# Second attention of a two-layer kernel: when the input's maximum and q's turn are issued, and which engines scale the output

## The reference

```python
def _dyn_quant(x):
    s = max(max(abs(x), axis=-1) / 127, EPS)
    return clip(round(x / s), -127, 127), s
def _w8a8_linear(x, w, b):
    qx, sx = _dyn_quant(x); qw, sw = _quant_weight(w)
    return einsum('bnc,oc->bno', qx, qw) * (sx * sw) + b
q = _w8a8_linear(layernorm(x), wq, bq)        # 16 heads of 32
k, v = ctx @ wk.T + bk, ctx @ wv.T + bv       # 64 keys
o = softmax(q k / sqrt(32) + mask) v
x = x + tanh(g_xattn[1]) * _w8a8_linear(o, wo, bo)
```

## Time and profile before

| what | value |
|---|---|
| median of three runs | 1836.82 us (1828.48 to 1837.65) |
| the profiled execution | 1837.09 us, of which 1835.3 us is the span of the trace |
| PE busy | 1727.9 us, 94% of the span |
| DVE, ACT, POOL busy | 1159.5, 1047.1, 971.2 us |
| first to last start of a scores matmul (S) | 1474.9 to 1605.1 us |

### The profile page before, as it was taken

The page is one execution under the profiler, slowest core; times in us unless marked ns, Lnnn a source line. Parts: engine busy times, 40 slices in busy tenths (PEclk is TensorE's granted clock), DMA queues, the critical chain, the costliest instruction groups (busy, mean ns, idle before and its releaser), DMA issues. The chain is left out here.

```text
span 1835.3 us, 28402 instructions
## 1 busy us (share of the span) xinstructions
PE 1727.9 (94%) x10014; PEld 1359.4 (74%) x10052; DVE 1159.5 (63%) x2436; ACT 1047.1 (57%) x2334; POOL 971.2 (53%) x864
## 2 busy tenths in 40 slices
PE   6999999999999999999998999989999878879998
PEld 4788888887877778777776888879999756634444
DVE  5666555557566675567666657644443768868886
ACT  3666666655655556555554421146656467858776
POOL 5654566545654457645531100038888446657774
PEclk9999999999999999999999999999999989999999
DMA  7121111101111111011222100167889770000000
GB/s 255 48 60 52 48 37 60 56 22 52 37 42 45 52 48 51 19 37 53 58 83 99 58 24 24 46 208 222 228 223 269 193 173 1 1 1 24 24 18 29
DMA packets 113611, 141.36 MB, mean 77 GB/s; under 512 B 38000, under 2 KB 68720, under 8 KB 113280
## 3 DMA queue, kind: packets, MB, share of 16 engines
q1 hardware_dynamic: 106304, 122.76, 21.2%
q0 software_dynamic: 7168, 16.78, 4.3%
HBM read 104.91 MB, written 29.36 MB: 73 GB/s over the span
## 5 line engine op out<-in xcount | busy, mean ns | idle before, releaser
L787 POOL TENSOR_TENSOR a_xcl<-xT,a_xch 128x512 fp32r<-128x512 f32 x64 | 86.1, 1346 | 335.4 <-ACT a_xch L571 335.4
L689 DVE TENSOR_REDUCE a_nmax<-a_S 128x1 f32<-128x192 f32 (+3 forms) x256 | 134.8, 548 | 49.3 <-PE a_S L897 49.1
L954 PE MATMUL a_A<-a_pT,a_vf 128*128 128x512 f32 x320 | 164.8, 597 | 0.3 <-ACT a_pT L592 0.3
L577 ACT ACTIVATE a_pr_odd<-a_S,a_nmax 128x320 f32<-128x320 f32 (+1 forms) x128 | 80.5, 630 | 120.5 <-DVE a_nmax L689 119.8
L120 PE MATMUL a_A<-a_wlo,a_xch 128*128 128x512 f32 x256 | 147.0, 574 | 1.2 <-DVE a_qT L685 1.2
L120 PE MATMUL a_S<-xl,xh 128*128 128x288 f32 (+3 forms) x320 | 122.5, 383 | 8.2 <-DVE xl L722 4.1
L2643 PE MATMUL f_HH<-w12T,f_f_xqT 128*128 128x512 bf16 x496 | 117.7, 383 | 10.7 <-DVE f_h L2496 7.8
L1619 POOL TENSOR_TENSOR e_wlo<-expert_raw,e_whi 128x1408 fp32r<-128x1408 f32 x31 | 101.0, 3260 | 50.4 <-ACT e_whi L1832 48.2
L577 ACT ACTIVATE a_pr_even<-a_S,a_nmax 128x192 f32<-128x192 f32 (+1 forms) x128 | 66.6, 523 | 103.5 <-DVE a_nmax L689 103.4
L120 PE MATMUL e_GUP<-e_xgl,e_whi 128*128 128x256 f32 (+1 forms) x384 | 110.7, 288 | 4.7 <-DVE e_xgl L1917 3.2
L714 DVE RECIPROCAL a_rec<-a_rs 128x1 f32<-128x1 f32 x256 | 41.2, 161 | 108.9 <-ACT a_pr_even L577 58.3
(11 more groups left out here) (443 smaller groups left out, 5576.5 us busy)
## 6 DMA issues: line engine op xcount, KB each, us to landing
a_pw<-in_L_ffn_w_dram SPq DMA_DIRECT2D x96, 256.0 KB, 2.8
expert_raw<-in_L_ffn_w_gate_dram SPq DMA_DIRECT2D x16, 704.0 KB, 8.0
expert_raw<-in_L_ffn_w_up_dram SPq DMA_DIRECT2D x16, 704.0 KB, 9.9
expert_raw<-in_L_ffn_w_down_dram SPq DMA_DIRECT2D x16, 512.0 KB, 10.3
tern<-a_tern SPq DMA_DIRECT2D x48, 128.0 KB, 1.7
x_res<-in_x_dram SPq DMA_DIRECT2D x4, 1024.0 KB, 9.1
a_raw<-in_L_xattn_wq_dram SPq DMA_DIRECT2D x4, 1024.0 KB, 5.9
a_raw<-in_L_xattn_wo_dram SPq DMA_DIRECT2D x4, 1024.0 KB, 5.5
```

The source lines that it names most:

```text
L577: act.activation(pr[s % 2][:, i, 0:keys(s)], pair(s, i), ACT.Exp, bias=nmax[:, s % 2, i:i + 1], accum_out=rs[:, s % 2, i:i + 1]).then_inc( ...
L689: ve.tensor_reduce(nmax[:, s % 2, i:i + 1], pair(s, i), AX.X, ALU.max, negate=True).then_inc(s_max, 1)
L787: pool.tensor_tensor(xcl[:, t % 2], xT[:, :, tok(t)], xch[:, t % 2].bitcast(F32), ALU.subtract).then_inc(xlo_ready, 1)
L954: pe.matmul(bank, vf[:, par(t), i], pT[:, i % 2], start=i == 0, stop=False)
```

## The change

Ahead of the slots, ACT quantises the second tile and centres the third only after it has scaled q of the first; DVE copies the first tile's turned input before the second maximum, and no longer takes the third tile's maximum, which falls to slot 0. In the slots, m works one tile later and stands behind M, x stands last; K stands ahead of V0 and T last on PE; k stands ahead of q, c and v on ACT. The maximum's home moves from PSUM to SBUF, so V0 no longer waits for it. The output of tiles 0 to 11 is scaled by row on ACT (step Y, first in the slot, tile s-3) and by weights on POOL, in step A, which moves from s-2 to s-3 and first multiplies, then waits for its own result, then adds. Tiles 12 to 15 keep the DVE form. Semaphores `y_act`, `y_pool` and `y_dve` take the place of `y_ready`; N waits for `y_act` before it writes `so` anew.

```diff
                 quantise_input(0)
-                quantise_input(1)
                 copy_weight(4)
-                centre(2)
                 act.wait_ge(q_full, 1)
                 act.activation(qs[:], QY[:], ACT.Identity, scale=sx[:, 0]).then_inc(qs_ready, 1)
+                quantise_input(1)
+                centre(2)
                 act.wait_ge(q_turned, 1)
...
                 values(0)
+                input_copy(0)
                 maximum(1)
                 statistics(2)
-                input_copy(0)
                 values(1)
                 input_copy(1)
-                maximum(2)
                 copy_weight(7)
...
-    PE_ORDER = "S0 U0 P0 Q0 P1 V0 K0 T0 V1 Y0"
-    ACT_ORDER = "q0 t0 i0 t1 c0 v0 k0 e0 O0"
-    DVE_ORDER = "D0 o0 M0 b0 x0 N0 Y0 m0"
+    PE_ORDER = "S0 U0 P0 Q0 P1 K0 V0 V1 Y0 T0"
+    ACT_ORDER = "Y0 t0 i0 t1 k0 q0 c0 v0 e0 O0"
+    DVE_ORDER = "D0 o0 M0 m0 b0 N0 x0"
     AHEAD = {"PE": {"T": 2, "Q": 1, "K": 1, "S": 0, "P": -1, "V": -1, "U": -2, "Y": -2},
-             "ACT": {"c": 3, "v": 3, "q": 2, "i": 1, "k": 1, "e": 0, "t": -1, "O": -1},
-             "DVE": {"b": 3, "m": 3, "x": 2, "D": 0, "M": 0, "N": -1, "o": -2, "Y": -2},
-             "POOL": {"B": 2, "p": 3, "s": 0, "A": -2}}
+             "ACT": {"c": 3, "v": 3, "q": 2, "i": 1, "k": 1, "e": 0, "t": -1, "O": -1, "Y": -3},
+             "DVE": {"b": 3, "m": 2, "x": 2, "D": 0, "M": 0, "N": -1, "o": -2},
+             "POOL": {"B": 2, "p": 3, "s": 0, "A": -3}}
...
                16: "U0.14 P0.15 Y0.14 P1.15 V0.15 fP1.0 V1.15 fT0.1 fP2.0 U0.15 fP3.0 Y0.15"}
-    ACT_JOIN = {10: "q0.12 t0.9 i0.11 t1.9 c0.13 v0.13 k0.11 G0.0 e0.10 O0.9",
-                11: "q0.13 t0.10 i0.12 t1.10 c0.14 v0.14 k0.12 H0.0 e0.11 O0.10",
-                12: "q0.14 t0.11 i0.13 t1.11 c0.15 v0.15 k0.13 H1.0 e0.12 O0.11",
-                13: "q0.15 t0.12 i0.14 t1.12 fc0.0 fv0.0 k0.14 e0.13 O0.12",
-                14: "t0.13 i0.15 t1.13 fc0.1 fv0.1 k0.15 e0.14 O0.13 fq0.0 fq1.0",
+    ACT_JOIN = {10: "Y0.7 t0.9 i0.11 t1.9 k0.11 q0.12 c0.13 v0.13 G0.0 e0.10 O0.9",
+                11: "Y0.8 t0.10 i0.12 t1.10 k0.12 q0.13 c0.14 v0.14 H0.0 e0.11 O0.10",
+                12: "Y0.9 t0.11 i0.13 t1.11 k0.13 q0.14 c0.15 v0.15 H1.0 e0.12 O0.11",
+                13: "Y0.10 t0.12 i0.14 t1.12 k0.14 q0.15 fc0.0 fv0.0 e0.13 O0.12",
+                14: "Y0.11 t0.13 i0.15 t1.13 k0.15 fc0.1 fv0.1 e0.14 O0.13 fq0.0 fq1.0",
                 15: "t0.14 t1.14 e0.15 O0.14",
                 16: "t0.15 fs0.0 t1.15 fq0.1 fq1.1 fs1.0 fz0.0 O0.15 fs2.0 fz1.0 fs3.0 fz2.0 fc0.2 fv0.2 fz3.0 fa0.0"}
-    DVE_JOIN = {13: "D0.13 o0.11 M0.13 fb0.0 x0.15 N0.12 Y0.11",
+    DVE_JOIN = {13: "D0.13 o0.11 M0.13 m0.15 fb0.0 N0.12 x0.15",
                 14: "D0.14 o0.12 M0.14 fb0.1 N0.13 Y0.12 fm0.0",
                 16: "o0.14 fg0.0 Y0.14 fg1.0 N0.15 fx0.1 fg2.0 o0.15 fb0.2 fg3.0 Y0.15 fH0.0 fH1.0 fH2.0"}
-    POOL_JOIN = {13: "B0.15 s0.13 fy0.0 A0.11 fy1.0 fp0.0",
-                 14: "s0.14 fy0.1 A0.12 fy1.1 fp0.1",
+    POOL_JOIN = {13: "B0.15 s0.13 fy0.0 A0.10 fy1.0 fp0.0",
+                 14: "s0.14 fy0.1 A0.11 fy1.1 fp0.1 A0.12",
                  15: "s0.15 A0.13",
     TINY = 1e-4
+    ACT_OUT = NT - 4
     NC = F1 // 512
...
         STAT = 2 * D1 + 2
-        am, mx, amo, mo = O[:, 0, STAT:STAT + 2], O[:, 1, STAT:STAT + 2], O[:, 2, STAT:STAT + 2], O[:, 3, STAT:STAT + 2]
+        am, mx, amo = homes["am"], homes["mx"], O[:, 2, STAT:STAT + 2]
         sc_full, sc_read, max_ready, centred, exp_done = (s_.sem(n) for n in ("sc_full", "sc_read", "max_ready", "centred", "exp_done"))
-        p_turned, p_copied, o_full, o_ready, oq_ready, oq_turned, oq_copied, y_full, y_ready = (s_.sem(n) for n in (
-            "p_turned", "p_copied", "o_full", "o_ready", "oq_ready", "oq_turned", "oq_copied", "y_full", "y_ready"))
+        p_turned, p_copied, o_full, o_ready, oq_ready, oq_turned, oq_copied, y_full, y_act, y_pool, y_dve = (s_.sem(n) for n in (
+            "p_turned", "p_copied", "o_full", "o_ready", "oq_ready", "oq_turned", "oq_copied", "y_full", "y_act", "y_pool", "y_dve"))
         biased, x_done, turned = s_.sem("biased"), s_.sem("x_done"), s_.sem("turned")
...
                     if name == "A":
-                        pool.wait_ge(y_ready, s + 1)
+                        if s < ACT_OUT:
+                            pool.wait_ge(y_act, s + 1)
+                            pool.tensor_tensor(y[:, u], y[:, u], gsw[:], ALU.mult).then_inc(y_pool, 1)
+                            pool.wait_ge(y_pool, s + 1)
+                        else:
+                            pool.wait_ge(y_dve, s + 1 - ACT_OUT)
                         pool.wait_ge(biased, s + 1)
...
                         act.activation(oq[:, u], o[:, u].rearrange("p j h d -> p (j h d)"), ACT.Identity, bias=big[:], scale=reco[:, u]).then_inc(oq_ready, 1)
+                    if name == "Y":
+                        act.wait_ge(y_full, s + 1)
+                        if s > 1:
+                            act.wait_ge(x_done, s - 1)
+                        act.activation(y[:, u], QY[:], ACT.Identity, scale=so[:, u]).then_inc(y_act, 1)
                     if name == "G":
...
                         link(ve.tensor_reduce(amo[:, u:u + 1], o[:, u].rearrange("p j h d -> p (j h d)"), AX.X, ALU.max, apply_absolute_value=True))
+                        if 1 < s < ACT_OUT + 2:
+                            ve.wait_ge(y_act, s - 1)
                         link(ve.tensor_scalar(so[:, u], amo[:, u:u + 1], 1.0 / 127.0, FLOOR, ALU.mult, ALU.max))
...
                             ve.wait_ge(x_done, s - 1)
-                        ve.scalar_tensor_tensor(y[:, u], QY[:], so[:, u], gsw[:], ALU.mult, ALU.mult).then_inc(y_ready, 1)
+                        ve.scalar_tensor_tensor(y[:, u], QY[:], so[:, u], gsw[:], ALU.mult, ALU.mult).then_inc(y_dve, 1)
                     if name == "b":
+                        ve.wait_ge(x_done, s + 1)
                         link(ve.bn_stats(f_stats[:, u], x[:, s]))
...
                         name, s = QY_LAST[name, s]
-                        pe.wait_ge(qs_ready if name == "Q" else y_ready, s + 1)
+                        if name == "Q":
+                            pe.wait_ge(qs_ready, s + 1)
+                        elif s < ACT_OUT:
+                            pe.wait_ge(y_act, s + 1)
+                        else:
+                            pe.wait_ge(y_dve, s + 1 - ACT_OUT)
...
                             pe.wait_ge(o_ready, s)
-                        if n == 0 and s + 3 < NT:
-                            pe.wait_ge(m_ready, 2 * (s + 4))
                         if n == 0 and s >= NT - 2:
...
                         elif n == 0:
-                            pe.wait_ge(y_ready, NT)
+                            pe.wait_ge(y_dve, NT - ACT_OUT)
                         for k in (range(Y_HEAD), range(Y_HEAD, F1 // P))[n]:
```

More of the change, by code:

```diff
@@ L2775, in turn_weights @@
                 sp.wait_ge(turned, 96)
-            homes = {**attention1_ffn1_homes(nc, kept, weights, sb), **{n: front[n] for n in ("cx", "xq", "xqT", "qs", "qT", "stats", "mv", "var", "root", "unroot", "rec", "sx")}}
+            homes = {**attention1_ffn1_homes(nc, kept, weights, sb), **{n: front[n] for n in ("cx", "xq", "xqT", "qs", "qT", "stats", "mv", "var", "root", "unroot", "rec", "sx", "am", "mx")}}
             attention1_ffn1_stage(nc, x, x_loaded, ident, gates, wT, sq, bq, gsw, gbo, mask, kbd, vbd, g12, g3, w12T, w3T, at, out, turn_weights, homes, front_sems)
```

## The result

The changed kernel takes 1839.87 us (median of 18 runs, 1835.45 to 1843.83); the kernel before, run 18 times beside it, takes 1834.41 (1828.48 to 1837.89). The ratio is 1.0029 with a 95% interval of 1.0019 to 1.0040: 0.3% slower, where 0.3% faster was forecast. It lies outside the range given, 1824 to 1838, though inside the half per cent that was called the same.

What follows compares the result with a forecast made beforehand. It took a two-slot chain of waits (DVE's list, c, k, S, PE's list) as the bound. Terms -2.6 - 2.9 + 0.5 = -5.0 on 1837.1 gave 1832.1, adjusted to the median 1831.8 us; range 1824 to 1838.

Steps and rivals of the forecast that it cites:

- Term 3: Twelve slots of the second attention: nine at 7.93 us, three with a g vector at 8.78; -2.9 us.
- The chain through the output: In each slot, U, Q, i, K, V0, V1, N, O in series to the next U; 7.93 us.
- The chain along ACT: In each slot, K then k, q, c, v, e and O in series on ACT; 7.83 us with the hand-over.
- DVE without Y works 6.8 us a slot, below 7.9: In the slots, DVE's work without the output scaling fits within the new slot time: 6.8 against 7.9 us.
- Two of its links go: Old two-slot chain in the slots: Y leaves DVE, 0.67 us a slot, and k no longer stands behind c.
- the slower rival: In the slots, POOL sets the pace because A's pair costs more than worked out; about 1853 us, chance 0.10.
- Term 1: Ahead of the slots: DVE's wait for PE's turn goes and the third maximum moves to slot 0; -2.6 us.
- DVE ends last: Ahead of the slots, DVE was taken as the last engine to finish, so shortening its work gains 2.6 us.
- Term 2: First two slots: k comes forward but T waits for q; 0, with bounds of 0.81 us either side.
- a clock away from 0.68: Sign in the first two slots: the prediction is wrong if the granted clock there is not near 0.68.
- Term 4: The join, slot 14: U to N takes 4.86 us where it took 4.40; +0.5 us.
- From there on ... 0: After N in slot 14, DVE's list is unchanged and POOL's late steps finish before they are wanted; 0.

Runs made afterwards that it cites:

- run 18: Not a run's label but a count: the kernel before was run 18 times beside the changed kernel; median 1834.41 us.
- E1: Changed kernel with sx taking its constant as a number, so one SBUF tensor instead of two; 1831.35 us against 1833.17 before, ratio 0.9989.
- E2: Kernel before with only the maximum's home moved from PSUM to SBUF; one run, 1832.95 us beside a median of 1833.17.
- E10: E8 with the copy x ahead of Y on DVE; 1832.12 us against 1833.00 before, ratio 0.9986.
- E7: Kernel before, old orders, with output scaling on ACT and POOL, maximum in SBUF and sx as in E1; 1832.19 us against 1834.56, ratio 0.9984.
- E5: Changed kernel with the edits of E1 and E4 together; 1829.74 us against 1833.17 before, ratio 0.9973.
- E11: E10 plus the edits of E4, E6 and E9, no scaling on ACT or POOL; 1825.24 us against 1833.00 before, ratio 0.9955.
- E4: Changed kernel with the third tile's two powers on POOL moved behind the barrier; 1836.47 us against 1833.17 before, ratio 1.0015.
- E8: E1 with all tiles' output scaled on DVE, Y behind N and ahead of x; 1836.53 us against 1834.56 before, ratio 1.0004.
- E3: Changed kernel, sx still with two SBUF tensors, b put ahead of m on DVE; one run, 1834.98 us beside a median of 1834.56.
- E6: E5 with two g scalings on ACT moved from slots 11 and 12 to slot 15; 1828.07 us against 1834.56 before, ratio 0.9968.
- E9: E6 with PE's and ACT's lists of slot 14 in the old order; 1827.21 us against 1833.00 before, ratio 0.9967.

## Why the prediction was wrong, step by step

**Term 3, the twelve slots: -2.9 forecast, +3.2 measured.** The chain through the output was right, and not by luck of the sum. With `sx` mended (E1) K starts 2.49 us behind U (2.47 worked out), N 4.91 (4.86) and the next U 7.92 (7.93); slots 10 to 12 take 8.82 for 8.78, and the twelve 97.72 for 97.7. The chain along ACT is as long in E1: from k to O ACT has no idle time, and N's last result is there 0.04 us before O starts (1547.87 + 0.16 = 1548.03, 1548.07). Which of the two bounds the slot is not shown. The step that failed is "DVE without Y works 6.8 us a slot, below 7.9". It added the old durations and took away Y's, while one of the operations that stay had lost its home in PSUM: `sx` holds DVE 1.84 us (1548.11 to 1549.95) where such an operation holds it 0.11 (E1). The moved home was costed as a wait removed from V0 and in no other way; E2 shows the home to be enough for a long `sx`, E1 shows `sx` to be the whole of the loss.

**What a slot owes to which edit.** "Two of its links go" was true but more than needed. The new orders together, K ahead of V0 and k ahead of c, v among them, give 7.92 without the scaling, provided that x stands ahead of Y (E10); the scaling on ACT and POOL gives 8.05 in the old orders (E7); both give 7.92 (E1). Which of the new orders decides is not shown, since no run moves one of them alone.

**The steps on ACT and POOL held.** Y on ACT takes 0.67 us and is not late; A's pair takes 1545.64 - 1544.29 = 1.35 to the second start, for 1.36; POOL has 1.15 us of idle time left in a slot of 7.92 us (E1, ahead of the powers), for 1.05 (1.08, had the sum taken 8.39 - 7.93 = 0.46 for the shorter slot and not 0.49). POOL's length did not set the pace, so the slower rival was wrong in its mechanism; POOL does harm through an operation of DVE that it keeps standing.

**Term 1, the head: -2.6 forecast, +0.4 measured.** The edit did to DVE what was said: the 1.45 us wait and the third maximum went, 2.6 us together. The step that failed is "DVE ends last". Before the change, too, POOL's drain ended 0.2 us behind DVE's arrival (1466.6 + 6.08 = 1472.7, against 1472.5), so there was nothing to gain until it came earlier as well: in E5 and E11, where it did, the head is 14.77 us against 17.51 before. A barrier has as many arrivals as engines, and only those that show as busy were looked at.

**Term 2, the first two slots: 0 forecast, -0.4 measured** up to U(0), within the bounds given. The forecast had named a clock away from 0.68 there as a sign against it: from S(0) to S(2) after had 0.75, and 18.27 us for 19.36. In the first slot alone the clock was 0.68 or 0.69 in before, after, E2, E4, E5, E7, E8 and E11, and 0.80 to 0.82 in E1, E3, E6, E9 and E10. S(0) to S(1) in after and in E10, each in a fence of its own:

```profile
1472.49:1482.16 9.67, 6.54 (x20) 3.94 (x21) 5.15 (x8) 3.21 (x7) 5.62 (x4) 0.68 1.08 235
```

```profile
1474.24:1482.69 8.45, 5.32 (x20) 3.61 (x21) 4.31 (x8) 3.05 (x7) 5.62 (x4) 0.81 1.13 226
```

Up to the barrier, after, E1, E3, E8 and E10 are one program. Yet in E1, E3 and E10 the granted clock fell to 0.50 during a product of the step ahead (L1704, which took 8.78 us in these three and 7.09 in after and E8), the head took 18.65 or 18.66 us against 17.94 in after and E8, and the first slot was then the quicker one. So the clock changes at another place from execution to execution of the same code. The prediction's sentence from the Trainium skill, "TensorE: Matmul & The Clock Gate", Part 1, that the moment of the switch varies by execution, agrees with this.

**Term 4, the join: +0.5 forecast, +1.6 measured.** U to N took 4.91 for the 4.86 worked out, and E9 traces it to K's place. "From there on ... 0" failed: N(13) to N(14) took 10.95 where it took 9.82, at a mean clock of 0.84 where it had 1.00. The window in before:

```profile
1601.72:1611.54 9.82, 7.27 (x52) 5.57 (x52) 8.22 (x16) 6.67 (x13) 8.25 (x8) 1.00 0.01 2
```

In PE's timeline of after the feed-forward's first turn shows the fall:

```profile
1608.58 1.04 PE L2666 MATMUL f_TB<-f_ident_h,f_f_xq 128*128 128x128 f16 x8 [2.10 <-ACT f_f_xq L2373]
```

PE has stood 2.10 us, and the turn takes 1.04 us where it takes 0.62 at full clock (E11, with a gap of 1.77). What makes the clock drop stays open. The length of that gap alone does not decide: E5 kept the clock behind 2.04 us and E7 behind 2.08, while E9 lost it behind 1.56. It dropped in eight of the ten profiles with the new order of the slots and in none of the three with the old one (before, E2, E7), but E5 and E1 have the same program from the barrier on but for the powers, and one kept the clock while the other lost it; and the old order in slot 14 alone (E9) did not save it.

**The rest of the sum.** +0.4 - 0.4 + 3.2 + 0.5 + 1.1 - 0.4 (N(14) to the end) gives 4.4 us, of the 5.5 between the medians.

## What to carry to other kernels

Before moving a small tile from PSUM to SBUF, look at every operation that reads it: one that then has two SBUF tensors as inputs may stand still for as long as POOL's operation runs (here 1.92 us for 0.20), and a row of the same operation from before no longer prices it; a number, or a scalar operand, in place of the second tensor avoids that. Ahead of a barrier, list each engine's arrival, drains included, and take the latest: here POOL arrived 5 us after its last visible work. And when a change moves both orders and work, try the orders alone: here they gave the whole slot once one copy was put ahead.

## What the runs showed of the hardware

- A DVE operation on 128 x 1 values, 0.197 us with its first input in PSUM, took up to 1.92 us with two SBUF tensor inputs, and ended within 0.02 us of POOL's running operation both where it started beside it and where it started 1.25 us into it. With the per-row factor as a scalar operand and one SBUF tensor it took 0.196 us beside the same POOL operations.
- POOL's drain at a barrier ended about 5.0 us after the end of its last two powers, wherever they stood: 1467.69 to 1472.7 before, 1465.31 to 1470.3 after, and 1461.89 to 1466.8 in E4, where they were the second tile's.
- The scatter between the runs of one kernel goes with the granted clock. Of the 18 runs of after, the three shortest (1835.45 to 1835.94 us) have a mean clock of 0.988 to 0.989 and the three longest (1843.38 to 1843.83) 0.981: 8 us, more than the whole effect of the change.
